# The state product of a Mamba-2 layer in three fp32r passes instead of one fp32 product

## What is computed

```python
xBC = jax.nn.silu(conv)                    # x, B and C of each token
dtx = dt_p[..., None] * x
def step(state, inp):
    dA_t, dtx_t, B_t, C_t = inp
    state = state * dA_t[..., None, None] + dtx_t[..., None] * B_t[:, :, None, :]
    y_t = jnp.einsum('bhpn,bhn->bhp', state, C_t)
    return (state, y_t)
y = jnp.moveaxis(ys, 0, 1) + x * D[None, None, :, None]      # the skip term
yn = (yg * lax.rsqrt(var + EPS)).reshape(B, L, I) * norm_weight
yn = yn * jax.nn.silu(gate)
out = jnp.einsum('bli,di->bld', yn, out_proj_w)
```

## Time and profile before

| | |
|---|---|
| median of 3 runs | 1791.78 us (1790.74 to 1792.49) |
| profiled execution | 1791.13 us, span 1789.3 us |
| TensorE matmul busy | 1757.7 us, 98% |
| TensorE weight loads busy | 1416.3 us, 79% |
| VectorE busy | 1523.1 us, 85% |
| GpSimd busy | 1145.7 us, 64% |
| ScalarE busy | 836.0 us, 47% |

### The profile page before, as it was taken

The page is one execution under the profiler, slowest core; times in us unless marked ns, Lnnn a source line. Parts: engine busy times, 40 slices in busy tenths (PEclk is TensorE's granted clock), DMA queues, the critical chain, the costliest instruction groups (busy, mean ns, idle before and its releaser), DMA issues.

```text
span 1789.3 us, 30683 instructions
## 1 busy us (share of the span) xinstructions
PE 1757.7 (98%) x11416; PEld 1416.3 (79%) x11416; DVE 1523.1 (85%) x1936; ACT 836.0 (47%) x1923; POOL 1145.7 (64%) x1143
## 2 busy tenths in 40 slices
PE   8999999999999999999999999999999999999997
PEld 5777888888888888888778788888888888888875
DVE  7879888898988889888888988889898888989887
ACT  4564453544445353443534444354443445444465
POOL 6447466475756657575697847658474764857567
PEclk9999999999999999999999999999999999999999
DMA  8533333232333323233574423333233332324234
GB/s 266 159 126 118 118 114 123 95 119 95 118 119 105 131 95 118 95 113 132 168 230 136 138 101 122 106 104 128 78 125 111 123 114 95 123 90 130 95 112 148
DMA packets 113508, 220.78 MB, mean 123 GB/s; under 512 B 10448, under 2 KB 46672, under 8 KB 113360
## 3 DMA queue, kind: packets, MB, share of 16 engines
q1 hardware_dynamic: 112320, 218.66, 36.8%
q10 hardware_dynamic: 1040, 0.16, 0.1%
HBM read 204.63 MB, written 14.16 MB: 122 GB/s over the span
## 4 chain that ended last, share of the span: by engine, by line
PE 83%; DVE 8%; ACT 4%; issue 2%; POOL 2%; DMA 1%; SPq 0%; ACTq 0%; DVEq 0%; POOLq 0%
PE ps_conv L1307 9%; PE ps_conv L1310 9%; PE ps_y L1486 6%; PE ps_conv L1313 6%; PE ps_out L1307 6%; PE ps_out L1310 6%; PE ps_gate L1307 6%; PE ps_gate L1310 6%; PE ps_y L1491 5%; PE ps_s L1523 5%; PE ps_out L1313 4%; PE ps_gate L1313 4%; PE turned_x L1403 3%; DVE xc L888 2%; PE ps_conv L1314 2%
## 5 line engine op out<-in xcount | busy, mean ns | idle before, releaser
L888 DVE SCALAR_TENSOR_TENSOR xc<-ps_conv,convw_sb,xc 128x511 f32<-128x511 f32 (+2 forms) x576 | 430.5, 747 | 154.0 <-ACT xc L654 140.5
L1240 POOL TENSOR_TENSOR rstd_col<-mean_square,half 128x1 f32<-128x1 f32 x128 | 88.8, 693 | 534.3 <-ACT mean_square L797 534.3
L1012 DVE TENSOR_TENSOR_SCAN decay<-decay,eye 128x1024 f32<-128x1024 f32 x125 | 294.3, 2354 | 0.0
L660 ACT ACTIVATE xc<-xc 128x512 f32<-128x512 f32 x192 | 121.1, 632 | 322.2 <-DVE xc L888 320.6
L1229 POOL TENSOR_TENSOR cpre<-cpre,xc 128x1024 f32<-128x1024 f32 x112 | 268.7, 2399 | 0.0
L1307 PE MATMUL ps_conv<-xn_hi,wconv_hi 128*128 128x512 f32 x768 | 241.9, 437 | 0.0
L1310 PE MATMUL ps_conv<-xn_hi,wconv_lo 128*128 128x512 f32 x768 | 207.4, 392 | 0.0
L1486 PE MATMUL ps_y<-decay,dtx 128*64 128x128 f32 x1984 | 190.9, 279 | 3.6 <-DVE decay L1033 2.8
L1307 PEld LDWEIGHTS ps_conv<-xn_hi,wconv_hi 128*128 128x128 f32 x768 | 141.4, 194 | 49.3 <-issue 27.4
L806 ACT ACTIVATE square<-ps_y 128x512 f32<-128x512 f32 x126 | 75.6, 600 | 219.0 <-DVE ps_y L1065 219.0
L1491 PE MATMUL ps_y<-cpre,state 128*64 128x128 f32 x1760 | 171.3, 273 | 0.0
(11 more groups left out here) (250 smaller groups left out, 3861.6 us busy)
## 6 DMA issues: line engine op xcount, KB each, us to landing
decay<-decays_d SPq DMA_DIRECT2D x125, 512.0 KB, 5.3
cpre<-rows_d SPq DMA_DIRECT2D x112, 512.0 KB, 4.0
stage<-w_in_t SPq DMA_DIRECT2D x32, 1024.0 KB, 6.6
stage<-w_out_t SPq DMA_DIRECT2D x16, 1024.0 KB, 5.5
stage<-w_in_t SPq DMA_DIRECT2D x32, 256.0 KB, 3.2
out_sum<-hidden SPq DMA_DIRECT2D x16, 256.0 KB, 5.7
ffn_d<-sgate SPq DMA_DIRECT2D x16, 256.0 KB, 3.2
out<-out_sum SPq DMA_DIRECT2D x16, 256.0 KB, 3.3
```

The source lines that it names most:

```text
L888: e.scalar_tensor_tensor(acc[:, d:], ps[:, 0:BLK - d], convw_sb[:, tile, TAPS - 1 - d:TAPS - d], acc[:, d:], ALU.mult, ALU.add).then_inc(S ...
L1012: e.tensor_tensor_scan(d, d, eye8[:, :, :].rearrange("p h i -> p (h i)"), 0.0, ALU.mult, ALU.add).then_inc(scanned(i)[0], 1)
```

## The change

In 98 of the 112 chunks that have one, the state product becomes three fp32r passes. ScalarE writes b_hi (from PSUM, beside b_tok) and xw_hi, GpSimd writes b_lo and xw_lo. The skip term of chunks 0 to 119 moves from GpSimd (one instruction) to ScalarE (four copies with a scale). The low halves of the weights are placed anew in GpSimd's order, most of them behind cpre. The diff without the allocations and the semaphores' names:

```diff
+def split_state(i):
+    return i < SCALED_XW and i % NCH < NCH - 1 and finished(i) is None
...
@scalar
+                    if split_state(i):
+                        e.activation(b_hi[:, :], ps_g[:, 0:P], ACT.Copy)
                     e.activation(b_tok[:, :], ps_g[:, 0:P], ACT.Copy).then_inc(S["b_tok"], 1)
...
+                if split_state(i):
+                    w.wait_ge(S["xw"], inner(i))
+                    w.wait_ge(S["mm_u"], inner(i) - 1)
+                    e.activation(xw_hi[:, :], xw[:, :], ACT.Copy).then_inc(S["xw_hi"], 1)
...
+                if i < SCALED_XW:
+                    w.wait_ge(S["silu"], max(conv_no(i // CPB, t) for t in range(XT)) + 1)
+                    w.wait_ge(S["par"], 128)
+                    w.wait_ge(S["y"], i)
+                    w.wait_ge(S["biased"], TOK)
+                    for t in range(XT):
+                        tile = g % GROUPS * XT + t
+                        done = e.activation(skip[:, t * P:(t + 1) * P], xc[i // CPB % 2][:, t, block_cols(i % NCH)],
+                                            ACT.Copy, scale=dskip_sb[:, tile:tile + 1])
+                    done.then_inc(S["skip"], 1)
...
@gpsimd
-                    if at == 1:
-                        split_out(g, range(XT))
-                    if at == 3 and left:
-                        split_conv_x(g + 1, range(KT))
-                    if at == 4 and left:
-                        split_gate(g + 1, (0, 1))
-                    if at == 5 and left:
-                        split_conv_bc(g + 1, range(KT))
-                    if at == 6 and left:
-                        split_gate(g + 1, (2, 3))
-                if i < N and i % NCH > 0:
-                    left_of_state(i)
+                if split_state(i):
+                    w.wait_ge(S["b_tok"], inner(i))
+                    e.tensor_tensor(b_lo[:, :], b_tok[:, :], b_hi[:, :].bitcast(F32), ALU.subtract).then_inc(S["b_lo"], 1)
+                if i < N and at == 1:
+                    split_out(g, (0,))
+                if split_state(i):
+                    w.wait_ge(S["xw_hi"], split(i))
+                    e.tensor_tensor(xw_lo[:, :], xw[:, :], xw_hi[:, :].bitcast(F32), ALU.subtract).then_inc(S["xw_lo"], 1)
+                if i < N and at > 0:
+                    left_of_state(i)
+                if i < N and at == 1:
+                    split_out(g, (1, 2, 3))
+                if at == 4 and left:
+                    split_gate(g + 1, (0,))
+                if at == 5 and left:
+                    split_conv_bc(g + 1, range(KT))
+                if at == 6 and left:
+                    split_gate(g + 1, (2, 3))
...
+                if at == 5 and left:
+                    split_gate(g + 1, (1,))
-                if i < N:
+                if SCALED_XW <= i < N:
...
+                if at == 2 and left:
+                    split_conv_x(g + 1, (0, 1, 2))
+                if at == 3 and left:
+                    split_conv_x(g + 1, (3,))
@tensor
-                    e.matmul(ps_s[:, :], b_tok[:, :], xw[:, :], start=True, stop=True).then_inc(S["mm_u"], 1)
+                    if split_state(i):
+                        w.wait_ge(S["b_tok"], inner(i))
+                        w.wait_ge(S["xw_hi"], split(i))
+                        e.matmul(ps_s[:, :], b_hi[:, :], xw_hi[:, :], start=True, stop=False)
+                        w.wait_ge(S["b_lo"], split(i))
+                        e.matmul(ps_s[:, :], b_lo[:, :], xw_hi[:, :], start=False, stop=False)
+                        w.wait_ge(S["xw_lo"], split(i))
+                        e.matmul(ps_s[:, :], b_hi[:, :], xw_lo[:, :], start=False, stop=True).then_inc(S["mm_u"], 1)
+                    else:
...
```

More of the change, by code:

```diff
@@ L77, in gated, with split @@
     return range(i + CPB - 1, min(i + CPB, N)) if i > 0 else ()
+def split_state(i):
+    return i < SCALED_XW and i % NCH < NCH - 1 and finished(i) is None
+def split(i):
+    return sum(split_state(k) for k in range(i + 1))
 def linear_at(s):
@@ L191, in build @@
         xw = sb("xw", [P, GC])
+        xw_hi = sb("xw_hi", [P, GC], F32R)
+        xw_lo = sb("xw_lo", [P, GC], F32R)
         b_tok = sb("b_tok", [P, NS])
+        b_hi = sb("b_hi", [P, NS], F32R)
+        b_lo = sb("b_lo", [P, NS], F32R)
         square = sb("square", [P, GC])
@@ L241, in build @@
             landed_rows0 landed_rows1 st_rows10 st_rows11 st_rows00 st_rows01
-            mm_t dtx scan last xw mm_bt b_tok mm_g M skip cpre mm_gate sgate mm_in mm_u
+            mm_t dtx scan last xw xw_hi xw_lo mm_bt b_tok b_lo mm_g M skip cpre mm_gate sgate mm_in mm_u
             y state sdec square sum1 sum2 mm_ssq var2 rstd2 yg hi2 lo2 mm_out osum
@@ L1240, in _ @@
                     e.tensor_tensor(rstd_col[:, col], mean_square[:, col], half[:, :], ALU.pow).then_inc(S["rstd2"], 1)
[L1241 to L1257 removed]
+                g, at = divmod(i, NCH)
+                if split_state(i):
+                    w.wait_ge(S["b_tok"], inner(i))
+                    e.tensor_tensor(b_lo[:, :], b_tok[:, :], b_hi[:, :].bitcast(F32), ALU.subtract).then_inc(S["b_lo"], 1)
+                left = i < N and BATCH * GROUPS - 1 - g
+                if i < N and at == 1:
+                    if g == 0:
+                        w.wait_ge(S["last"], inner(i))
+                    split_out(g, (0,))
[3 more added lines that the diff above has]
+                if i < N and at > 0:
+                    left_of_state(i)
+                if i < N and at == 1:
[6 more added lines that the diff above has]
+                    split_gate(g + 1, (2, 3))
                 if 0 <= m < N:
[L1259 removed]
                     w.wait_ge(S["square"], m + 1)
@@ L1264, in _ @@
                     e.tensor_tensor(square_sum[:, :], square[:, 0:P], square[:, P:2 * P], ALU.add).then_inc(S["sum2"], 1)
+                if 0 <= m < N:
+                    bm, cm, gm = batch(m), m % NCH, group(m) % GROUPS
                     if cm < NCH - 2:
@@ L1519, in _ @@
                     w.wait_ge(S["pt"], 3 if i < 3 else 4)
-                    w.wait_ge(S["b_tok"], inner(i))
-                    w.wait_ge(S["xw"], inner(i))
                     w.wait_ge(S["state"], inner(m) if m >= 0 else 0)
-                    e.matmul(ps_s[:, :], b_tok[:, :], xw[:, :], start=True, stop=True).then_inc(S["mm_u"], 1)
+                    if split_state(i):
[7 more added lines that the diff above has]
+                    else:
+                        w.wait_ge(S["b_tok"], inner(i))
+                        w.wait_ge(S["xw"], inner(i))
+                        e.matmul(ps_s[:, :], b_tok[:, :], xw[:, :], start=True, stop=True).then_inc(S["mm_u"], 1)
                 if i < N and conv_late(i) is not None and not late_first:
@@ L1559 @@
     }
-    nc = bacc.Bacc("TRN2", target_bir_lowering=False, num_devices=1)
+    nc = bacc.Bacc("TRN2", target_bir_lowering=False, num_devices=1, dynamic_dma_scratch_size=1024)
     args = [nc.dram_tensor(name, a.shape, mybir.dt.from_np(a.dtype), kind="ExternalInput").ap()
```

1 line of the change is left out of this document (removed).

## The result

The changed kernel takes 1816.43 us (median of 4 runs, 1816.17 to 1816.66), the one before 1791.26 in the same session. The ratio is 1.0142, with a 95% interval of 1.013 to 1.0155: 1.4% slower, +25.2 us, where +12 were forecast. The profiled execution took 1816.35 us, its span 1814.5.

The account below looks back on a forecast made before the run. TensorE, without gaps, was taken to bound the kernel: -18.4 (shorter product) + 19.6 and + 13.5 (stalls at positions 1 and 3) - 3 (finishing chunks) = +11.7 us, so 1803 us. The 8-in-10 range was 1783 to 1817.

Parts of the forecast that it names:

- three passes: TensorE's state product: three fp32r passes save 0.17 to 0.20 us a chunk, 1.3 per group, 18.4 in all.
- skip pieces, c: ScalarE, behind the gate's SiLU below chunk 120: four scaled copies add 1.1 us per chunk.
- The coarser rule: Trainium skill's ACTIVATE budget for the skip pieces: 0.41 us each, 1.6 a chunk, about 1817 us in all.
- Position 0 to 1: ScalarE's serial chain runs late, so TensorE waits for xw_lo at position 1: 1.4 us in 14 groups, +19.6.
- GpSimd and SyncE: GpSimd gets 0.7 us more a chunk, low halves mostly hidden; SyncE's weight fetches make nothing late.
- Position 2 to 3: ScalarE's late taps delay the mixing matrix, so TensorE waits at position 3: 0.9 us in 15 groups, +13.5.
- The scan beside state: VectorE's scan of position 2 collides with GpSimd's state: 0.3 us, partly covered, inside the 0.9 at position 3.
- The finishing chunks: Around 900 to 1070 us GpSimd has less to do, relieving TensorE's idle time: -3 us, between 0 and -5.
- only one stall forms, or none: Rivals at positions 1 and 3: one stall gives 1790 us, chance 0.1; none gives 1770, within a joint 0.2.
- heavier: Rival: skip pieces don't overlap (1.5 us a chunk) or the scan is held 1.04: 1815 us and up, chance 0.1.

Follow-up runs that it names:

- e5: The changed kernel with the last three wout_lo tiles ahead of cpre on GpSimd at position 1; 1804.53 us.
- e2: The kernel before with only the skip term moved to ScalarE as four scaled copies; 1809.85 us.
- e1: The changed kernel with the skip term back on GpSimd as one instruction; 1801.14 us.
- e3: e1 without b_lo and xw_lo: the state product is b_hi by xw_hi three times; 1773.63 us.
- e4: The changed kernel with each chunk's skip pieces moved to the next iteration, between the late conv's first tap and its SiLU on ScalarE; 1787.53 us.
- e7: The changed kernel with xw_lo ahead of the first wout_lo tile on GpSimd; 1829.14 us.
- e8: e4 with GpSimd's order at position 1 made b_lo, xw_lo, four wout_lo tiles, cpre; 1781.24 us.
- e9: e4 with b_hi, b_tok and mean_square ahead of the four wout_hi roundings on ScalarE at position 1; 1777.78 us.
- e10: e9 with all wout_lo tiles ahead of cpre on GpSimd, as in e5; 1773.86 us.

## Why the prediction was right in direction and off in size

By the prediction's steps, per group in the changed kernel:

| step | predicted | measured |
|---|---|---|
| three passes | -1.31 | -1.43 |
| skip pieces, c (no term of the sum; it is in the stalls) | 1.1 | 1.17 |
| stall for xw_lo, position 1 | 1.4 | 1.54 |
| stall for wout_lo, position 2 | none | 0.85 |
| stall for the mixing matrix, position 3 | 0.9 | 0.78 |
| sum | +1.0 | +1.76 |

The twelve groups 1 to 6 and 9 to 14 give 12 x 1.79 = +21.5. The first gives +3.0, the two with finishing chunks (7 and 8) +0.8 together, the last -0.4, and +0.4 stands ahead of the first chunk: +25.2 with rounding.

**The three passes** were right in kind and 0.12 a group too small: 0.23 and 0.17 where 0.20 and 0.17 were read.

**c = 1.1** measured 1.17 us; the group of all 480 pieces in the changed kernel:

```profile
L852 ACT ACTIVATE skip<-xc,dskip_sb 128x128 f32<-128x128 f32 x480 | 153.8, 405 | 0.0
```

One piece is 405 ns long in the mean, but the pieces overlap, and occupy 1.17/4 = 293 ns each. The Trainium skill (ScalarE: Activation LUTs, What ACT_TABLE_LOAD costs) has a finer rule than the one that the prediction quoted: 186 ns, 93 more for an operand from memory, 0.833 ns an element, and an overlap of about 93 between neighbours. By it a piece is 386 ns long and occupies 293. This trace agrees: 5% more in the length, and the same in what a piece occupies. The coarser rule's 1.6 us, and the 1817 us worked out from it, had the cause wrong although the time is near: it has c too high and the wait for wout_lo not at all.

**Position 0 to 1** is right: ScalarE's chain has no slack. rstd_col stands 1.50 late in the group, less the 0.17 explained above 1.33, against 1.25 predicted, and TensorE waited for xw_lo where and how long it was said. e5 leaves 1.31 + 0.23 = 1.54 of this stall alone.

**The step that failed** is "GpSimd and SyncE". It followed the three wout_lo tiles behind cpre to what stands behind them (square_sum, state, the scan) and to SyncE's next fetches, and ended in "so nothing is late". It never asked who reads the tiles themselves. That is the output projection on TensorE in position 2, whose third pass multiplies wout_lo. The old trace had the tiles done at 653.14 and that pass some 3.6 us later; c, b_hi, b_lo, xw_lo (1.25) and cpre (2.4) put 5.6 us ahead of the end of the last tile, 2.0 more than the room. TensorE itself comes 1.3 later by then (1.54 for xw_lo, less 0.23), so 0.7 should be left. The runs showed +0.85 us a group in place of nothing: e5 takes it away and gains 11.9 us, 13 x 0.85 = 11.0 of it in the groups. By groups, the 13.5 us that the forecast was short are 12 x 0.8 = 9.6 in the full groups, 2.0 in the first (open, see below) and 1.9 in groups 7 and 8 (+0.8 for -1.1). In a full group wout_lo's 0.85 is more than the whole difference; the small errors of the other terms nearly cancel.

**Position 2 to 3** is right in the changed kernel (0.78 for 0.9), and for the reason given: ScalarE waits for TensorE at the gate's SiLU, so one c counts. That this alignment is itself a product of the stalls ahead the prediction did not see; e2 showed it, with 1.21.

**The scan beside state**: it took 2.55 instead of 2.28 us at position 2, 0.27 for the 0.3 taken. state itself fell from a mean of 1353 ns to 1046 (longest 3.03 us before, 1.05 now), so it no longer runs beside a scan.

**The finishing chunks**: the relief is in group 7, whose columns 3-4 and 4-5 are -0.89 and -1.90, 2.8 us together for 3 predicted. The reason given is not needed in both its parts: e1 and e3 have the skip back on GpSimd and show the same (-0.87 and -1.90), while the skip moved alone (e2) gives -0.87 and -0.63. What e1 and e3 share with the changed kernel there are the new places of the weights' low halves; no run moved these alone. Group 8 gives back 0.9 more than its terms: TensorE waited 1.99 us for the state at 985.2, and the granted clock was 0.66 from 985 to 990.

**The rivals.** That only one stall forms, or none, is refuted; "heavier" gave the right time for a wrong reason (c was 1.17, and the scan lost 0.27). The real rival was missing: a second wait on the same GpSimd queue.

**Open**: in the first group column 0-1 is +4.05, 1.9 more than elsewhere. The waits show TensorE idle 2.8 us for the state (L1104), and the granted clock is 0.76 from 130 to 135 us. What made the state late there was not traced, and no experiment isolates it. The clock seems to be part of it: behind this same wait it fell in the changed kernel, e1, e4, e5, e7 and e8, and stayed up in e2, e3, e9 and e10, where the column is smaller (+1.15, +0.61, +2.73, +1.89, against +3.39 and more). Why it fell in these, and in four groups of e7 and not in the others, stays open.

## What to carry to other kernels

When an instruction is moved back in a queue, list who reads its result before who stands behind it, and compare the time at which each reader wants it with the new end; a queue of six jobs has six deadlines, and mending one of them alone (e7) only hands the stall to the next. Where the bound engine waits for a chain, the same work can differ by 29 us by its place in that chain (e4 against the change), so look for the slot in which its engine waits anyway before asking which engine should do it. Stalls are not additive: one realigns the engines and hides another, so a part tested alone may cost more than its share in the whole.

## What the runs showed of the hardware that was not expected

- A GpSimd instruction on one column took 1.61 us instead of 0.55 when it started beside VectorE's scan (e9), and the skip of 512 columns took 3.02 instead of 1.04 in e1, beside the scan of position 2, as state did in the earlier trace rows. The Trainium skill (SBUF — State Buffer, Who interferes with whom) says that the two contend only through the pair of ports that they share, and that this is an exclusive lock. The lengths agree with waiting for the rest of the scan: 1.26 us of it was left in e9 and 2.19 in e1, and the instructions took 1.06 and 1.98 longer. No run here varied that alone.
- TensorE's granted clock went to the lower level 0.5 to 1.1 us behind the end of a stall of 1.8 us in four groups of e7, and stayed up in the other nine that have the stall, where it was 1.76 to 1.82 us long. In the first group it fell behind a stall of 2.44 us (e4) and stayed up behind one of 2.53 (e9). So the length of the stall alone does not decide it. In e7 the cost was 1.6 us each, nearly that of the stall itself.
